# One value product of the last directed layers taken off VectorE, all engine orders rewritten, other set-up: six fused graph layers on one Trainium2 core

## What is computed

```
x += GAT(relu(ln(x)), adj)             # layer 0: 12 heads, masked softmax
x += two directed layers (DIR_A, DIR_B)  # layers 1, 2: exp(h W_left h^T), W_right, W_lin, std layer norm, relu
x += two directed layers (DIG_A, DIG_B)  # layers 3, 4:
    a    = softmax(h h^T / sqrt(D)) * adj, rows normalised
    ctx  = (a upper) @ (h Wl^T + bl) + diag(a) * (h Ws^T + bs) + (a lower) @ (h Wr^T + br)
    h    = relu(layernorm(ctx) * g + beta)
x += Graphormer(relu(ln(x)), adj)      # layer 5: 12 heads, adj as bias, output projection
```

## Time and profile before

| | us |
|---|---|
| median of 3 runs | 2855.91 (2854.23 to 2859.2) |
| the profiled execution, device time | 2849.21 |
| its span, first to last instruction | 2847.5 |
| TensorE busy in it | 2677.8 (94%) |
| VectorE busy | 2469.1 (87%) |
| ScalarE busy | 1950.6 (69%) |
| GpSimd busy | 1444.1 (51%) |

### The profile page before, as it was taken

How to read it: one execution, slowest core, us unless ns; L and a number is a source line. 1 busy time by engine, 2 the same in 40 slices (tenths; PEclk the granted TensorE clock), 3 DMA queues, 4 the chain that set the end, 5 groups by cost and what they waited for, 6 DMA issues and landing times. The chain is left out here.

```text
span 2847.5 us, 85381 instructions
## 1 busy us (share of the span) xinstructions
PE 2677.8 (94%) x32384; PEld 2026.1 (71%) x32384; DVE 2469.1 (87%) x6758; ACT 1950.6 (69%) x6740; POOL 1444.1 (51%) x2345
## 2 busy tenths in 40 slices
PE   5799999999999999999999999999999999999996
PEld 4567777777777777777777777777777777776764
DVE  7788898889888898889888888889898888988885
ACT  7466676676766676677676767677677667676653
POOL 4644554454544454555554544455455555555543
PEclk9899999999999999999999999999999999999998
DMA  8232333332332333233332332332332332332220
GB/s 214 78 64 55 56 65 56 55 65 57 58 61 54 55 67 56 55 66 55 57 64 56 59 61 54 56 67 56 53 67 53 57 66 54 57 66 53 56 43 20
DMA packets 546323, 175.69 MB, mean 62 GB/s; under 512 B 513665, under 2 KB 545665, under 8 KB 545665
## 3 DMA queue, kind: packets, MB, share of 16 engines
q1 hardware_dynamic: 536704, 157.64, 30.5%
q10 hardware_dynamic: 9216, 12.59, 1.3%
HBM read 31.72 MB, written 12.58 MB: 16 GB/s over the span
## 5 line engine op out<-in xcount | busy, mean ns | idle before, releaser
L981 PE MATMUL bank<-w_hi,ht 128*128 128x384 f16 x3840 | 1043.8, 327 | 0.0
L981 PE MATMUL bank<-ht,w_hi 128*128 128x128 f16 x9216 | 823.5, 221 | 21.9 <-DMA ht<-qk 16.5
L981 PE MATMUL bank<-ht,w_lo 128*128 128x128 f16 x4608 | 801.0, 221 | 0.0
L981 PEld LDWEIGHTS bank<-ht,w_hi 128*128 128x128 f16 x9216 | 724.1, 99 | 96.4 <-issue 53.2
L981 PE MATMUL bank<-w_lo,ht 128*128 128x384 f16 x1920 | 628.2, 327 | 0.0
L719 ACT ACTIVATE t<-t,few 128x128 f32<-128x128 f32 x1536 | 593.8, 391 | 7.4 <-POOL qk L605 1.6
L981 PEld LDWEIGHTS bank<-w_hi,ht 128*128 128x128 f16 x3840 | 376.6, 98 | 234.0 <-issue 15.1
L981 PEld LDWEIGHTS bank<-ht,w_lo 128*128 128x128 f16 x4608 | 454.6, 99 | 0.0
L591 POOL TENSOR_TENSOR h<-h,row 128x384 f32<-128x384 f32 x256 | 256.6, 1002 | 158.5 <-DVE h L960 158.5
L797 DVE TENSOR_TENSOR qk<-bank,qk 128x256 f16<-128x256 f32 x576 | 234.4, 418 | 106.8 <-ACT qk L710 106.3
L719 ACT ACTIVATION_READ_ACCUMULATOR t<-t,few 128x1 f32 x1536 | 292.8, 191 | 0.0
(11 more groups left out here) (122 smaller groups left out, 5428.2 us busy)
## 6 DMA issues: line engine op xcount, KB each, us to landing
x<-in_x_dram SPq DMA_DIRECT2D x64, 192.0 KB, 2.3
out_dram<-h ACTq DMA_DIRECT2D x64, 192.0 KB, 1.9
ht<-qk SPq DMA_TRANSPOSE x384, 2.8
w_hi<-in_weights_dram SPq DMA_DIRECT2D x9, 576.0 KB, 5.2
w_lo<-in_weights_dram SPq DMA_DIRECT2D x8, 576.0 KB, 5.3
adj<-in_adj_dram SPq DMA_DIRECT2D x64, 64.0 KB, 2.2
row<-in_rows_dram SPq DMA_DIRECT2D x1, 1920.0 KB, 9.6
row<-in_rows_dram SPq DMA_DIRECT2D x1, 1536.0 KB, 10.2
```

What stands on the lines that cost most here:

```text
L981: m = nc.tensor.matmul(out, a, b, start=(first and n == 0), stop=(last and n == 3 * len(left) - 1))
```

## The change

Value (DIG_B, 2), that is layer 4's third, leaves `VALS_ON_VECTOR`: once for each graph. It is evicted by ScalarE and gets its bias from GpSimd. In the set-up, the weights 5 and 8 and the eight bias rows are centred by ScalarE instead of GpSimd. All strings of all five engines are new; the strings of SP's BODY hold the same cyclic order, begun at another place.

```diff
-VALS_ON_VECTOR = ((DIG_A, 0), (DIG_A, 1), (DIG_A, 2), (DIG_B, 0), (DIG_B, 1), (DIG_B, 2))
+VALS_ON_VECTOR = ((DIG_A, 0), (DIG_A, 1), (DIG_A, 2), (DIG_B, 0), (DIG_B, 1))
...
+CENTRED_BY_SCALAR = (5, 8)
...
 BODY = {
     "tensor":
-        "032311212211000330434331221312321122404414433143422323322111441040442332423432233010020044204033"
...
+        "232031121221010303304343121231321122240441443343142232332121414410404232342432233301002004404203"
...
             def set_up():                                   # GpSimd
                 for k, w in enumerate(CENTRED_W):
+                    if w in CENTRED_BY_SCALAR:
+                        continue
...
-                    if k == 0:
-                        pool.wait_ge(row_sums, 2)
-                        for n in range(8):
-                            nc.gpsimd.tensor_scalar(row[:, 1 + n], row[:, 1 + n], means[:, n:n + 1], None,
-                                                    ALU.add).then_inc(rows_centred, 1)
-                        yield
...
             def set_up():                                   # ScalarE
-                    if w in CENTRED_W:
-                        act.wait_ge(w_centred, C * (CENTRED_W.index(w) + 1))
+                    if w in CENTRED_BY_SCALAR:
+                        k = CENTRED_W.index(w)
+                        act.wait_ge(w_sums, 2 * k + 2)
+                        for c in range(C):
+                            nc.scalar.activation(stage_of(w)[:, c], stage_of(w)[:, c], ACT.Identity,
+                                                 bias=means[:, 8 + k * C + c:9 + k * C + c]).then_inc(first_centred, 1)
+                        act.wait_ge(first_centred, C * (CENTRED_BY_SCALAR.index(w) + 1))
+                    elif w in CENTRED_W:
+                        act.wait_ge(w_centred, C * (CENTRED_W.index(w) + 1 - len(CENTRED_BY_SCALAR)))
...
+                    if w == 4:
+                        act.wait_ge(row_sums, 2)
+                        for k in range(8):
+                            nc.scalar.activation(row[:, 1 + k], row[:, 1 + k], ACT.Identity,
+                                                 bias=means[:, k:k + 1]).then_inc(rows_centred, 1)
+                        yield
```

More of the change, by code:

```diff
@@ L129 @@
     "tensor":
-        "032311212211000330434331221312321122404414433143422323322111441040442332423432233010020044204033"
-        "434433222002101003443034043344121131100310144040044333113212114004140104400232242211421200101100"
-        "444224323220110201210011343303322",
+        "232031121221010303304343121231321122240441443343142232332121414410404232342432233301002004404203"
+        "343443232020021010343403043344412113110010314404004343131132121404014104400023224221121420010110"
+        "404242243232010120210011134330332",
     "vector":
[L134 to L137, removed]
+        "322002044032111234424121113320343434212422312334230023241420424331131001432223400302322244314040"
+        "403230334234403411343020310304422421120433340114134333004201010143414403400140224041314214100330"
+        "322310444012202404441103121212040200140112013301024203202114414334210001233130100022142323231013"
+        "1120122312441213031431",
     "scalar":
-        "023100241134421000323143131342143112311240334404224104013421130224003211143420424240320422342230"
-        "144001033021012403224133011432220403103030143103340334120011214413212301433024412204333101421414"
-        "12042144014402311223200243234120441300233104442120320202310320012001342233431130434",
+        "034100124134420321003143313113442311122124033440422410341402112302400314321142044242240034222332"
+        "301440010330214020132234130114204322031003033011403334434120011214413201312433402412203104331421"
+        "1414412201444004023112232002431242304401302331421044203220200233120001101342233431130423",
     "pool":
-        "003230221134233232214114341332240344343320220402443301400404431331013004412011010042442124110023"
-        "122121103",
+        "003232201143322323221411434331220443343433202204044233100440404431331010034421100101004244212114"
+        "00322112121103",
     "sync":
-        "33132010344424312140003042320111410343122202140423",
+        "20103444243121400030423201114103431222021404233313",
 }
@@ L154 @@
+        "22223032110120200111333330322322212111133333223322211112113333332222233333322222333332333333",
     "vector":
[L155 to L158, removed]
@@ L159 @@
-        "33323",
+        "322002044230211132444122333111324342041231432331023002444224324123310103321422340032042234241404"
+        "303302403144243114300033230302244124241033430114134340320301104013414420300402214011344413431032"
+        "230004144020120444041121314120202002410113210321203020421013131213230003101002102233213120311021"
+        "221233312313101222233221112112131333232123233323122233232333132232222333333333232233333333323",
     "scalar":
-        "032001112443204100231331314311321131244203430444122401043114200023241311032424422422430042412323"
@@ L165 @@
+        "2321111233213223322323332322332222223333333333133023",
     "pool":
-        "003232211343232312241143413302024434343320224004433100404044333121013004241101100202214110023212"
-        "21131233202133323122233323233313323",
+        "003230221134332321224231144133224044334330322204024433010404044341333101004412100101002221110230"
+        "211212131403232213332132222333233233331323",
     "sync":
-        "331320103444241321000430243210114130432221021032331321323233",
+        "20103444241321400030423201114103431222021023331321323233",
```

31 lines of the change are left out of this document (15 added, 16 removed).

## The result

The changed kernel takes 2888.4 us (median of 4 runs, 2888.1 to 2892.2) against 2855.1 for the kernel before (median of 4): a ratio of 1.0123, interval 1.0103 to 1.0143. It is 33 us slower, where 33.5 us less were forecast (2822, range 2786 to 2855). The profiled execution took 2888.1 us (span 2886.4), 38.9 more than the one of before.

The account below looks back on a forecast made before the run. The prediction took GAT's mix waiting for its send DMAs, 1.02 us a turn, as the bound. Body -29, set-up 0, opening -5, end +0.5 gave -33.5 from 2849.2: 2815.7, or a median of 2822, range 2786 to 2855.

Parts of the forecast that it names:

- What bounds the kernel: The whole machine runs to one wait: GAT's mix for the landing of the send DMAs, 1.02 us a turn.
- Part 1: TensorE takes proj2.2 before mix, so gram1 could end 1.00 us sooner; at most 1.02 a turn, 65 us in all.
- Part 2: First half of the turn: after 0.35 of new waits, gram1 starts on VectorE 0.65 earlier after mix (bounds 0, 1.00).
- The walk: Turn worked through step by step: VectorE's second half of mix5 some 0.5 later, context4 0.5 earlier, cnorm2 some 0.1 earlier.
- the loss of 0.35 to new waits: TensorE's new small waits at aturn2, flips and context2 in the first half, put at 0.35 (bounds 0, 1.0).
- Part 3: Second half, from gram1 to the sends: ScalarE's different order costs net 0.2 a turn (bounds -0.5, +0.7).
- Part 2's list: Where TensorE would meet new small waits: aturn2 and flips, 1.0 to 2.6 us earlier, and context2, needing vals2.
- Part 4: Set-up: GpSimd loses eight row operations and two weights' centring, ScalarE gets them at about 0.70 each; 0 (bounds +5, -5).
- Part 5: Opening and closing: -5 us for the opening (bounds -15, +8), +0.5 us for the end of the run.
- (b): GpSimd's moved addition gets in the way of VectorE's mix5, 0.14 a turn, 9 us: 2831; chance 0.12.
- (c): New waits eat the gain, the body stays as before, 2850 to 2860; chance 0.13.
- (d): ScalarE becomes the bound of the second half; VectorE's last splits and the sends slip, 2869; chance 0.09.

Follow-up runs that it names:

- e5: Kernel before with only TensorE's proj2.2 moved ahead of scores0 and mix; 2861.0 us, ratio 1.0016.
- e3: Changed kernel with TensorE's proj2.2 behind the mix again, all else as changed; 2925.6 us, ratio 1.0236.
- e1: Changed kernel with GpSimd's addition for cnorm2 ahead of the moved value's bias addition instead of behind it; 2866.9 us, ratio 1.0024.
- e12: e1 with GpSimd's addition for the moved value replaced by a zero fill of the same block; 2836.8 us, ratio 0.9946.
- e10: e9 with ScalarE taking vals5, proj0.1 and proj0.2 ahead of proj2.0; 2818.7 us, ratio 0.989.
- e7: Kernel before with the change's set-up alone, the last layers' weights centred by ScalarE; 2858.2 us, ratio 1.0019.
- e8: e2's BODY behind the opening and set-up of the kernel before; 2841.9 us, ratio 0.9953.
- e2: Changed kernel with the moved value on VectorE again, just ahead of context4, TensorE's order untouched; 2848.6 us, ratio 0.9971.
- e14: e1 with the TensorE moves of e9 and the ScalarE order of e10; 2842.6 us, ratio 0.995.
- e9: e8 with TensorE's proj0.2 ahead of proj2.0 and the entering load ahead of aturn1; 2854.3 us, ratio 0.9988.
- e11: e1 with ScalarE's half of mix5 ahead of the eviction of vals4.2; 2868.8 us, ratio 1.0064.
- e13: Changed kernel, in its own order, with GpSimd's addition for the moved value replaced by a zero fill; 2862.5 us, ratio 1.0029.

## Why the prediction was wrong

**What bounds the kernel.** Right up to the mix: proj2.2 ahead of it removes its wait. Wrong in calling it one cycle through gram1, VectorE's 21 steps and the sends. A second piece closes it: mix, TensorE's steps to layer 5's mix (after the change to vals4.2), VectorE's row to proj1.2, gram1. It had no slack at all.

**Part 1** (at most 1.02 a turn): e5 shows it worth nothing without new cover for back0, and e3 shows it worth 0.60 a turn with the new order (43.98 against 43.38). TensorE's busy time, whose ends are modelled, is 41.54 a turn instead of 41.34 with only this step moved (e5) and 41.63 after the change; why, and whether it costs anything, isn't shown.

**Part 2** is the step that failed: gram1 was to come 0.65 earlier after the mix and came 0.18 later. Of these 0.83, the larger part is the sentence that VectorE "had 0.61 us to spare ahead of gram1". It read idle time on VectorE as slack without asking what TensorE had waited for. The same text put residual2 at "only some 0.1 earlier", and with a rigid row behind it gram1 could not gain more than that 0.1: 0.55 were booked that weren't there. The other 0.3 is residual2 itself, 0.21 later instead of 0.1 earlier. That is cnorm2's 0.33 by the collision with VectorE's mix5. mix5's own 0.49 lies hidden behind cnorm2, and comes to light in e1. The walk itself had mix5 right, "some 0.5 us later" (0.45), but let it keep its length. In e12, where neither an addition nor cnorm2's place behind it is left, gram1 came 0.76 earlier: TensorE's side of the walk, the loss of 0.35 to new waits, was not what failed.

**Part 3** forecast that the second half gives back 0.2; it was 0.49, and by another way. VectorE's row was not held up: its last split ends 13.45 us after gram1's start, before 13.61. The sends leave as early after the mix as before (35.4), and TensorE arrives after the landing: proj2.2's microsecond is now its work in this half in place of the mix's wait, and new waits at proj2.0 (0.32) and aturn1 (0.26, before 0.13) come on top. Part 2's list named aturn2, flips and context2. e10 shows the half can be had at 21.08, that is +0.12. Parts 2 and 3 together: 0.67 lost instead of 0.45 won. In the 55 turns of the eleven BODYs that is 1.12 x 55 = 62 us, of the 72 by which the profiled execution missed its 2815.7 (66 in the medians); the other 10 lie in the opening, the end and their turns.

**Part 4** (0, bounds -5 to +5): +5 in e7, at the bound, with an interval that begins at 0. No gain from GpSimd's relief shows. ScalarE's price was 0.52 a row, not 0.70. **Part 5**: the -5 for the opening did not come; e8 against e2 puts opening and set-up together at some +5, which the set-up alone would explain. BODY began at 190.2, not 181.

**The rivals.** (b) was true in its mechanism, mix5 took "near 1 us", and mis-sized: only a quarter of a meeting (0.14) was let through to the cycle, but 0.33 is on it, each turn, by way of cnorm2. e1 against e2, and e14 against e10, price the value behind cnorm2 at 0.35 and 0.33 of the first half. (c) is what the turn became, and worse. (d) did not happen: VectorE does not stop for ScalarE ahead of the splits. No rival had the moved value's detour itself on the loop, though the text had all its numbers: 0.48 and 1.01 in a row in place of 0.55.

## What to carry over

Idle time ahead of an instruction is slack only if what it waits for did not itself wait for this engine: follow the releaser one step further before booking it. In a loop of several engines, an operation taken off a full engine can cost more than it saves if its new path, two engines in a row and their queues, lies between two steps of the loop; count latency from the producer's end to the consumer's start, and what stands behind the newcomer in its queue. When a step moves on one engine, the eviction order of the others has to move with it (e9 to e10: 36 us for one reordering on ScalarE).

## What the runs showed of the hardware

A VectorE instruction with two SBUF inputs and a GpSimd addition hold each other up. mix5's half takes 0.56 us alone and 1.05 when it starts 0.36 into an addition: it ends 0.42 behind the addition's end. GpSimd's cnorm2, starting at that same end, while mix5 is still at work, takes 1.33 instead of 1.00. Where mix5 starts 0.42 ahead of the addition it has its old length (e11: 559 ns), and with cnorm2 ahead of the addition so has cnorm2 (e1: 1.00). Started together, mix5 takes 0.56 and cnorm2 1.42 (e13). The Trainium skill, page "SBUF — State Buffer", on the shared port pair, says that whichever instruction starts first holds the pair for its whole length. The trace agrees in order and nearly in size: in all three meetings (1.05, 1.33, 1.42) the later one ends 0.14 us sooner than if it had done all of its work after the earlier one. I had expected the meeting to be rare; in this order, which repeats, it happens in every turn (the mean of 46 is 1.054).

A GpSimd addition of 128 x 384 float32 takes 1.00 us, a fill of the same block 0.42.
